# First pair's low weights and bias ahead of the last early chunk of edges; its key reads ahead of the wait for the end of the value stage

## What is computed

```
qkv = xn @ w_qkv + b_qkv                # 12 heads of 64
A = (q * SCALE) @ k.T
w = 1 + A + 0.5 * A * A
attn = w / w.sum(-1);  out = attn @ v;  out @ w_proj + b_proj
GCN: out[dst] += (xn @ W)[src] * dinv[src] * dinv[dst]    # 20000 edges
FFN: top-1 switch routing to 8 experts with a capacity
```

## Time and profile before

| | us |
|---|---|
| runs shown, median (lowest, highest) | 1050.02 (1047.7, 1053.79) |
| the profiled execution, its own time | 1044.9 |
| its span, first to last instruction | 1043.2 |
| PE busy | 907.2 (87%) |
| DVE busy | 760.2 (73%) |
| ACT busy | 489.8 (47%) |
| mean granted TensorE clock | 0.947 |

### The profile page before, as it was taken

How to read it: one execution, slowest core, us unless ns; L and a number is a source line. 1 busy time by engine, 2 the same in 40 slices (tenths; PEclk the granted TensorE clock), 3 DMA queues, 4 the chain that set the end, 5 groups by cost and what they waited for, 6 DMA issues and landing times.

```text
span 1043.2 us, 15413 instructions
## 1 busy us (share of the span) xinstructions
PE 907.2 (87%) x5154; PEld 859.8 (82%) x5154; DVE 760.2 (73%) x1566; ACT 489.8 (47%) x720; POOL 361.5 (35%) x236
## 2 busy tenths in 40 slices
PE   2897789989989999999999896989999995499995
PEld 2897689879979988988988786888999995498884
DVE  6869249889888879889888685654566667467773
ACT  2211256665765766667567640251232332164640
POOL 1014546553544554553564610000000001425562
PEclk9999799999999999999999898999999996599998
DMA  9987362464364355346327349426676744577861
GB/s 275 349 142 192 56 126 30 63 112 79 62 111 80 50 99 89 65 81 107 65 25 160 51 88 186 107 56 173 167 195 176 188 155 134 165 220 243 259 216 46
DMA packets 137614, 136.70 MB, mean 131 GB/s; under 512 B 70561, under 2 KB 118276, under 8 KB 136545
## 3 DMA queue, kind: packets, MB, share of 16 engines
q1 hardware_dynamic: 109646, 119.29, 44.4%
q0 software_dynamic: 27520, 16.67, 11.5%
q10 hardware_dynamic: 403, 0.17, 0.1%
HBM read 94.31 MB, written 38.17 MB: 127 GB/s over the span
## 4 chain that ended last, share of the span: by engine, by line
PE 50%; DVE 20%; issue 12%; DMA 10%; ACT 5%; POOL 1%; SPq 1%; DVEq 0%; ACTq 0%; POOLq 0%
PE ps L1998 8%; PE ps L2000 7%; PE ps L1999 7%; PE ps L1175 7%; PE ps L1594 3%; PE ps L1159 3%; PE ps L1595 3%; PE ps L1160 3%; DMA out<-oE,ids 3%; DVE Pl L1034 3%; DMA vdram<-VS 3%; DVE Ph L1032 2%; DMA Cs<-counts 2%; ACT Ph L822 2%; DVE eqs L506 2%
## 5 line engine op out<-in xcount | busy, mean ns | idle before, releaser
L380 POOL DMA_INDIRECT counts<-countc,idxu x157 | 275.7, 1756 | 265.2 <-DMA counts<-countc,idxu 229.1
L1034 DVE SCALAR_TENSOR_TENSOR Pl<-Pf,Ph 125x832 fp32r<-125x832 f32 (+1 forms) x180 | 184.3, 1028 | 57.0 <-ACT Ph L822 52.8
L844 ACT ACTIVATE Pf<-ps 125x832 f32<-125x832 f32 (+1 forms) x180 | 156.1, 868 | 135.7 <-PE ps L1160 122.5
L1175 PE MATMUL ps<-Ph,vsb 125*128 125x416 f32 (+1 forms) x360 | 132.7, 369 | 22.1 <-DVE Pl L1034 22.0
L1175 PE MATMUL ps<-Pl,vsb 125*128 125x416 f32 (+1 forms) x360 | 128.3, 356 | 0.0
L1175 PEld LDWEIGHTS ps<-Ph,vsb 125*128 125x128 f32 x360 | 69.2, 192 | 34.7 <-DVE Pl L1034 20.6
L1998 PE MATMUL ps<-XH,wqkH 128*128 128x416 f32 (+1 forms) x216 | 83.2, 385 | 10.2 <-DVE wqkL L891 8.5
L1998 PE MATMUL ps<-wH,XH 128*125 128x384 f32 x240 | 84.3, 351 | 4.1 <-DVE wL L473 4.1
L1999 PE MATMUL ps<-wL,XH 128*125 128x384 f32 x240 | 82.6, 344 | 0.0
L2000 PE MATMUL ps<-wH,XL 128*125 128x384 f32 x240 | 82.6, 344 | 0.0
L822 ACT ACTIVATE Ph<-Pf 125x832 fp32r<-125x832 f32 (+1 forms) x90 | 80.5, 896 | 0.7
(11 more groups left out here) (274 smaller groups left out, 2191.9 us busy)
## 6 DMA issues: line engine op xcount, KB each, us to landing
Cs<-counts SPq DMA_DIRECT2D x20, 546.9 KB
w1s<-L_ffn_w SPq DMA_DIRECT2D x8, 1152.0 KB, 6.6
w2s<-L_ffn_w SPq DMA_DIRECT2D x8, 1152.0 KB, 6.1
odram<-OHL SPq DMA_DIRECT2D x12, 625.0 KB, 8.6
oS<-odram SPq DMA_DIRECT2D x10, 750.0 KB, 4.9
vdram<-VS SPq DMA_DIRECT2D x10, 672.0 KB
vsb<-vdram SPq DMA_DIRECT2D x12, 560.0 KB
kt<-keyd SPq DMA_DIRECT2D x5, 1280.0 KB, 6.1
```

The costliest lines, as they stand in the source:

```text
L380: pool.indirect_dma_start(out=counts, out_offset=bass.IndirectOffsetOnAxis(ap=idxu[:, c:c + 1], axis=0), in_=countc[:, c:c + 1], in_offset ...
L844: act.activation(Pf[:, i % RING, :, 0:w], ps[0:T, 2 * (i % 2):2 * (i % 2) + 2, 0:w], ACT.Square, bias=1.0).then_inc(sq_done, 1)
L1034: dve.scalar_tensor_tensor(out=p, in0=f, scalar=1.0, in1=h.bitcast(F32), op0=ALU.add, op1=ALU.subtract).then_inc(p_lo, 1)
L1175: ins = pe.matmul(ps[:, 4 + s % 2, 0:w], vsb[:, 2 * kp + t, a, :], part[:, m % RING, t, 0:w], start=(kp == 0 and t == 0 and part is Ph), s ...
```

## The change

DVE makes both low parts of the first pair's weights, and the bias columns, between `value_lo(9)` and `edge_chunk(6)`, by a new function `first_weights`; the three calls at the head of the second DVE block go. ACT waits for the 15 units of turned input (`tr_done`) and reads the three key groups before it waits in `values_over`, not after. No instruction of DVE, ACT or PE is added or dropped; one wait of ACT is new.

```diff
@@ -292,6 +292,14 @@
+        def first_weights(dve):
+
+            for s_ in (1, 0):
+                dve.wait_ge(wqk_hi, 2 - s_)
+                dve.tensor_tensor(wqkL[:, s_], ws[:, s_], wqkH[:, s_].bitcast(F32), ALU.subtract).then_inc(wqk_lo, 1)
+            dve.tensor_scalar(pbias[:], bcols[:, 0:2, 0:1].rearrange("p s o -> p (s o)"), 1.0, None, ALU.mult
+                              ).then_inc(bias_ready, 1)
+
         @block.sync
@@ -548,6 +556,8 @@
             for i in range(3, NT):
                 value_lo(i)
+                if i == NT - 1:
+                    first_weights(dve)
                 edge_chunk(i - FIRST_EDGES)
@@ -799,10 +809,11 @@
             split_w(0, 1)
             split_w(0, 0)
-            values_over(act)
+            act.wait_ge(tr_done, len(XUNITS))
             act.wait_ge(bias_ready, 1)
             for g in range(3):
                 read_kq(0, g)
+            values_over(act)
             split_w(1, 1)
@@ -926,9 +937,6 @@
-            split_w(0, 1)
-            split_w(0, 0)
-            pair_bias(0)
             dve.sem_inc(oacc_done, FREE)
             values_over(dve)
```

## The result

| | before | changed |
|---|---|---|
| median of 6 runs each, us | 1049.45 (1047.07 to 1059.0) | 1040.59 (1037.65 to 1043.27) |
| ratio, 95% interval | | 0.990 (0.9857 to 0.9943) |
| the profiled execution, its own time and span | 1044.9, 1043.2 | 1039.22, 1037.5 |
| mean granted clock of it | 0.947 | 0.952 |

The account below looks back on a forecast made before the run. PE's idle 8.52 us before the first pair held about six of comparisons on DVE that PE does not need. Forecast: 6.03 (seam) + 0.7 (clock) = 6.7 us off the median 1050.02, giving 1043.3 us; range 1039 to 1049.

Parts of the forecast that it names:

- the sum: Whole kernel: 6.03 us from the seam plus 0.7 from the clock, 6.7 less, taken from the median 1050.02.
- The clock's term: First key products after PE's shorter gap: fewer run at the slow clock, 0.7 us gained, bounds 0 and 1.4.
- The comparisons are what PE waited for: Between values and first pair: low weights ahead of the last comparisons let PE start at 100.53, not 106.56, 6.03 us earlier.
- The two subtractions' price on the chunk: Last comparison chunk on DVE: ends near 107.2, not 105.2, holding nobody; price nothing, or 1.95 us if uncovered.
- The reads cost nothing and keep part 1 whole: ACT's key reads ahead of `values_over`: no cost, and avoids reading 1.3 us late, 2.7 at the fast clock.
- part 1: DVE, between values and first pair: the low weights go ahead of the last chunk of comparisons, 6.03 us earlier for PE.
- POOL's chain holds: Pair stage: adding DMAs end near 606.0, before SP wants them at 607.6; cost nothing, bounds 0 and 6.
- 9.4 us of slack: End of the pairs: POOL's last adding DMA lands about 604.9, SP loads the counts at 614.31; the change uses 6.7.
- that rival: End of the pairs: the adding DMAs end last and cut the gain to 2.8 us, giving 1047.2; chance 0.18.
- its groups take 6.8 us in the pairs: POOL's adding DMAs: 5.7 us a group ahead of the pairs, 6.8 in them, so one more group falls into the pairs.
- Adding DMAs beside the low weights: POOL's issues during DVE's two subtractions: up to 1.9 us longer by the skill's rule, nothing by the rows; nothing taken.
- the prediction's own signs of being wrong: Changed profile: counts loaded at 609 or later by a landing, a K read waiting for idxu, or slow products from 100.5.

Follow-up runs that it names:

- e10_order: Changed kernel, with ACT rounding the first weights behind value tile 8, DVE's low weights ahead of tile 9's low values, both last chunks after: ratio 0.9918.
- e3_weights: Changed kernel, but with ACT's key reads left behind the wait for the end of the value stage: ratio 0.9944, mean 1041.1 us.
- e7_late14: Changed kernel with fourteen small DMAs, each waited for, ahead of POOL's first adding DMA: 1060.5 us in a single execution.
- e2_again: The changed kernel timed a second time against the kernel before, no edit: ratio 0.9929.
- e6_late4: Changed kernel with four small DMAs, each waited for, ahead of POOL's first adding DMA: ratio 0.9942, mean 1040.7 us.
- e1_same: The kernel before timed against itself, no edit: ratio 0.9985, median 1046.0 us.

## Why the prediction was right or wrong

The mechanism was right; what failed is a size. The step that failed is in the sum and its range: the difference was taken from a median of three executions, with "about 2.5 either way" for its spread. That median, 1050.02, was 2.3 us above the mean of the 101 later executions of the kernel before, and the comparison itself left an interval of 4.5 us either way. From the mean, the forecast's 6.7 would have given 1041.1, and the changed kernel's mean is 1040.7. The clock's term was mis-sized too, but that is not what moved the result.

- **The comparisons are what PE waited for, and the low weights can pass them** (6.03): right. Gaps of 8.2 to 8.5 became 2.4 to 3.6, in the mean of three and of four profiles 5.4 less; the term was high by half a microsecond, since the rounding and, in two executions, DVE's last low values were later than in the rows.
- **The two subtractions' price on the chunk is nobody's** (end near 107.2): right, 107.45. Also e10_order, where it is 112.1.
- **The reads cost nothing and keep part 1 whole** (1.3 to 2.7 if left): right; alone 1.0004, and 1.4 us of the seam in e3_weights.
- **No loss on the way; POOL's chain holds**: right. But "9.4 us of slack" and "by 1.6 us" came from one execution with the longest such chain of all; 21 us of delay were free. Read from several profiles, the chance of 0.18 for that rival would have been lower. That its groups take 6.8 us in the pairs however they start is also wrong: a chain begun 21 us later ended only 5 later than in the changed kernel's profile.
- **Adding DMAs beside the low weights, "by the rows nothing"**: wrong in the mechanism, without a price. See below.
- **The clock (0.7, from 0 to 1.4)**: mis-sized in the seam. In the changed kernel's profile the term was -0.3 (5.66 against 5.37), in the others from +1.2 to -1.3: the first group takes 4.12 to 6.71, in the mean 0.3 less than in the three profiles without the change. The slow products behind 100.90 are one of the prediction's own signs of being wrong, and the first key read, 5.65 us after PE's start, lies just outside its 4 to 5.5.
- **The seam and the whole**: the seam was 6.7 in the sum and is 5.9 in the first pair of profiles, 6.1 in the mean of three and four (40.95 to 34.85), of which 0.4 lies behind the first read, where the prediction saw only a possible loss. The whole kernel gives some 7 to 9. The remaining 1 to 3 us, which the sum put at nothing, are hardly larger than the uncertainty of the means (1.4 either way), and their place stays open: behind the first scores the profiles of the two kernels take 905.7 and 904.7 us in the mean, with single ones from 898 to 911. Part of them goes with the clock: the mean granted clock is 0.9463 over the 101 executions of the kernel before and 0.9495 over the 29 of the changed one. Within the first set 0.01 more clock goes with 6.3 us less time (correlation -0.78), so 0.0032 is 2.0 us, and the other 5.1 us are there at equal clock. Part of the 0.0032 is mere bookkeeping (the kernel before idles for 3.4 us at half clock in its gap, which is 0.0016 of its span), so the split leans on a correlation and is argued, not shown.
- **The range (1039 to 1049)**: 1040.59 lies in it, but the ratio puts the changed kernel at 1038.96 (0.990 of 1049.45), just below its low end. That end was made of the forecast's term and 2.5 us for the spread of a median of three runs. Six runs of each kernel, with the one at 1059.0, left an interval of 9 us; the range had no room for that. That 1040.59 came out 2.7 under the forecast is for the most part the luck of a high starting value, not more gain.

## What to carry to other kernels

Where an engine that makes an operand for TensorE has independent work in front of it, ask of the chain who waits for what, and move the operand's operation ahead by the length of that work; the consumer behind it (here ACT's read) must be freed of the same wait, or a part comes back. Slack against an outside chain of DMAs should be read from several executions or tried by delaying it. And with single runs that lie 12 us apart (standard deviation 3.1), the size of a gain of 6 is known to some 2 us only from twenty executions of each kernel on; its sign needs fewer.

## What the runs showed of the hardware

**Run-to-run scatter goes with TensorE's clock.** The pair stage, the same work in each profile, takes 469.8 us with 3.4 us of TensorE's work at 1.2 GHz in it and 475.5 to 476.6 with 17.1 us: 0.44 us for each. A line through all the profiles but e7_late14's gives 0.41 (correlation 0.94 over thirteen). Its granted clock, from the stretches (columns as above) of e3_weights and of e2_again:

```profile
135.10:604.90 469.80, 433.21 (x2257) 402.09 (x2257) 405.34 (x741) 316.44 (x453) 240.01 (x137) 1.00 0.44 77
```

```profile
135.40:612.00 476.60, 439.42 (x2257) 407.89 (x2257) 405.13 (x741) 316.56 (x453) 236.66 (x137) 0.98 0.43 76
```

The clock fell at gaps of 2.4 and 3.3 us in some executions and not at 2.9 and 3.6 in others: the gap's length alone does not decide. The Trainium skill (TensorE: Matmul & The Clock Gate, Part 1) says that the number of slow matmuls varies from run to run of one kernel; these runs agree, with none to some sixteen of the eighteen products of the first group.

**A subtraction on DVE did hold POOL's issue.** In the changed kernel POOL began an adding DMA at 99.93, behind the start of the low weights at 99.79 (timeline of POOL):

```profile
99.93 2.24 POOL L388 DMA_INDIRECT counts<-countc,idxu  x1 [2.12 <-DMA counts<-countc,idxu]
102.48 1.55 POOL L388 DMA_INDIRECT counts<-countc,idxu  x1 [0.30 <-issue]
```

It took 2.24 instead of 1.55; the three repeats show 2.03 to 2.11 in that position and e3_weights 1.76, while in the kernel before, and in e6_late4, an issue that began just ahead of the subtraction took 1.54 to 1.55. The change did not bring this: where an issue began inside the subtractions in the kernel before, it was held as well, as in e1_same (timelines of DVE and POOL):

```profile
105.45 1.83 DVE L891 TENSOR_TENSOR wqkL<-ws,wqkH 128x768 fp32r<-128x768 f32 x2 [0.25 <-DVE idxu L517]
106.42 2.28 POOL L380 DMA_INDIRECT counts<-countc,idxu  x1 [0.30 <-issue]
```

Twelve profiles have such an issue, and in each it ends 1.55 us behind one of two moments: 0.82 to 0.83 us after the first subtraction's start if it began in the first (seven), 1.69 to 1.70 after it if it began in the second (five). Each moment lies some 0.1 us ahead of the end that the trace gives for that subtraction. So POOL waits out the running subtraction and then does its whole work. DVE is not held: its two take 1.81 to 1.83 in every profile, also where POOL had begun first. The first half agrees with the Trainium skill (SBUF — State Buffer, Who interferes with whom), which says that a VectorE instruction with two SBUF inputs contends with a GpSimd one that reads SBUF, and that the order of issue decides who is blocked; a VectorE instruction blocked by an earlier GpSimd one is what no run here shows. The prediction held the rows against that rule, but its rows had POOL's issues only ahead of the subtraction or away from it.
